# Three edits around the slot loop: the order of GpSimd's diagonal adds, and where TensorE waits for a slot's low parts

## The reference

```python
x = x + einsum('bct,bcd->bdt', x, L0_weights[itok_B_0_15])      # 64x64 mix of the rows, one of 16
x = x + einsum('bct,bcd->bdt', x, L1_weights[itok_B_0_15])      # the same, other weights
x = x + einsum('bsi,oi->bso', x, W) + low_rank(x, lora_A[itok_B_0_2], lora_B_w) * 0.5
x = x + einsum('bsi,boi->bso', x, L3_weight[itok_B_3_7])        # 1024x1024 adapter, one of 8
```

## Time and profile before

| | us |
|---|---|
| median of 3 runs | 383.75 |
| lowest and highest | 383.16, 384.0 |
| the profiled execution, time of the run | 384.77 |
| its span, first to last instruction | 383.0 |
| granted TensorE clock, mean | 0.999 |

### The profile page before, as it was taken

One profiled execution on the slowest core, in us unless ns is written; L12 is line 12 of the kernel. 1 busy time (PEld: TensorE's weight loads), 2 busy tenths in 40 slices (PEclk: granted clock), 3 DMA queues, 4 the chain that ended last, 5 costly groups with the idle time before them and its releaser, 6 DMA issues.

```text
span 383.0 us, 7652 instructions
## 1 busy us (share of the span) xinstructions
PE 376.4 (98%) x1733; PEld 312.9 (82%) x1734; DVE 267.6 (70%) x301; ACT 225.5 (59%) x299; POOL 115.3 (30%) x157
## 2 busy tenths in 40 slices
PE   8999999999999999999999999999999999999995
PEld 7888888888888888888888888778888888888784
DVE  3796977847849788447968458844599635999653
ACT  3689577487247375244474565753677536778443
POOL 0000230100000000024765356663167532566600
PEclk9999999999999999999999999999999999999999
DMA  8975905630378294406528226542256522664223
GB/s 276 399 284 206 344 0 181 236 133 7 106 269 287 103 329 152 171 9 220 159 73 267 63 51 203 205 125 59 56 187 200 169 58 58 205 228 123 60 62 86
DMA packets 24187, 61.38 MB, mean 160 GB/s; under 512 B 1906, under 2 KB 2098, under 8 KB 24114
## 3 DMA queue, kind: packets, MB, share of 16 engines
q1 hardware_dynamic: 23648, 60.10, 47.6%
q10 hardware_dynamic: 466, 0.44, 0.3%
HBM read 52.15 MB, written 8.39 MB: 158 GB/s over the span
## 4 chain that ended last, share of the span: by engine, by line
PE 97%; DMA 1%; issue 0%; DVE 0%; ACT 0%
PE ps L1514 45%; PE ps L1373 12%; PE ps L1374 12%; PE ps L1375 12%; PE ps L1400 4%; PE ps L1537 4%; PE ps L1439 3%; PE ps L1602 2%; PE ps L1412 2%; DMA ring_f<-xt 1%; PE ps L1552 1%; PE ps L1449 0%; DVE ring L878 0%; ACT stage L850 0%
## 5 line engine op out<-in xcount | busy, mean ns | idle before, releaser
L1514 PE MATMUL ps<-ring,aT 128*128 x752 | 173.7, 390 | 0.5 <-issue 0.5
L1514 PEld LDWEIGHTS ps<-ring,aT 128*128 128x128 f32 x752 | 140.9, 188 | 30.8 <-issue 1.7
L1373 PE MATMUL ps<-ring 128*128 128x512 f32 x208 | 81.1, 390 | 0.0
L1374 PE MATMUL ps<-ring 128*128 128x512 f32 x208 | 81.0, 389 | 0.0
L1375 PE MATMUL ps<-ring 128*128 128x512 f32 x208 | 80.9, 389 | 0.0
L476 POOL TENSOR_TENSOR aT<-xT,aT 128x512 fp32r<-128x512 f32 (+1 forms) x36 | 56.4, 1587 | 46.3 <-ACT aT L761 43.1
L1266 DVE TENSOR_TENSOR ring<-raw,ring 128x1024 f32 (+1 forms) x40 | 62.6, 1623 | 6.2 <-ACT ring L747 6.2
L767 ACT ACTIVATE aT<-ps 64x1024 fp32r<-64x1024 f32 x32 | 32.7, 1023 | 47.1 <-PE ps L1514 46.7
L1294 DVE TENSOR_TENSOR stage<-ps,stage 64x1024 f32<-64x1024 f32 x30 | 36.7, 1222 | 29.4 <-ACT stage L776 28.7
L1283 DVE TENSOR_TENSOR aT<-ps,aT 64x1024 fp32r<-64x1024 f32 x32 | 39.1, 1223 | 21.6 <-ACT aT L767 20.9
L1375 PEld LDWEIGHTS ps<-ring 128*128 128x128 f32 x208 | 39.1, 188 | 8.2
(11 more groups left out here) (95 smaller groups left out, 328.6 us busy)
## 6 DMA issues: line engine op xcount, KB each, us to landing
raw<-w3t SPq DMA_DIRECT2D x40, 512.0 KB, 4.4
ring_f<-xt SPq DMA_DIRECT2D x8, 1024.0 KB, 8.4
raw<-xt SPq DMA_DIRECT2D x8, 1024.0 KB, 5.3
out<-stage SPq DMA_DIRECT2D x30, 256.0 KB, 3.2
ring_f<-wt SPq DMA_DIRECT2D x4, 1024.0 KB, 8.1
xT<-xt SPq DMA_DIRECT2D x3, 1024.0 KB, 10.4
xT<-wt SPq DMA_DIRECT2D x2, 1024.0 KB, 16.0
ring_f<-wt SPq DMA_DIRECT2D x4, 256.0 KB, 5.1
```

Of the source, the lines that this page charges most:

```text
L1373: pe.matmul(dst, hi_of(qw)[:, k, cs], hi_of(qx)[:, k, :], start=start and k == 0, stop=False, skip_group_check=True)
L1374: pe.matmul(dst, hi_of(qw)[:, k, cs], lo_of(qx)[:, k, :], start=False, stop=False, skip_group_check=True)
L1514: last = pe.matmul(acc(i)[:, n, :], x3_split(i, k, start, P), ring[:, bass.ds(off + (part * D + n * 512), 512)], start=(k == 0 and j == 0) ...
```

## The change

Two functions change. In GpSimd's `step`, the adds for MORE of slot i are no longer made in step i but in step i+1, after `slot_lo(i+2)` and `mixers(i+1)`; the adds for LOAD_A stay in their step (those of slot 0 are made in step 1, as before), and come after those for MORE where a step has both. On TensorE, `slot_ready` of slots 1 and on waits for the slot's high parts (`s_hi`) and no longer for its low parts; the wait for the low parts (`s_lo`) stands now ahead of the first matmul of tile 0 that reads them: the third pass of a pair, which is after 4 matmuls, and the first pass of a single batch.

```diff
-                for w in ([], [earlier, word])[i] if i < 2 else [word]:
-                    with pool.If(get(w, LOAD_A) > 0):
-                        adapter_eyes(HALF, pool.snap(get(w, THIS)))
-                    with pool.If(get(w, MORE) > 0):
-                        adapter_eyes(0, pool.snap(get(w, THIS) + 1))
+                if i == 1:
+                    with pool.If(get(earlier, LOAD_A) > 0):
+                        adapter_eyes(HALF, pool.snap(get(earlier, THIS)))
+                if i:
+                    with pool.If(get(earlier, MORE) > 0):
+                        adapter_eyes(0, pool.snap(get(earlier, THIS) + 1))
+                    with pool.If(get(word, LOAD_A) > 0):
+                        adapter_eyes(HALF, pool.snap(get(word, THIS)))
                 return word, following
@@ products, on TensorE
                     for j, (start, part) in enumerate(passes):
+                        if i and k == 0 and start + P > P and j == (len(passes) - 1 if start == P else 0):
+                            pe.wait_ge(s("s_lo"), 2 * i + 4)
                         for n in range(2):
@@ slot_ready, on TensorE
-                pe.wait_ge(s("s_lo"), 2 * i + 4 if i else 2)
+                if i:
+                    pe.wait_ge(s("s_hi"), 2 * i + 4)
+                else:
+                    pe.wait_ge(s("s_lo"), 2)
```

## The result

| kernel | median us | lowest to highest | runs |
|---|---|---|---|
| before | 383.75 | 383.16 to 384.13 | 5 |
| changed | 395.05 | 393.93 to 395.80 | 5 |

A forecast was written before the change was run, and what follows sets the result against it. TensorE, busy 98% of the span, was taken as the bound, so stalls count in full. Two places at 2.76 us plus 1.87 at slot 6's made 7.4, added to the 383.75 median: 391.2 us, range 388.4 to 394.6.

The forecast's parts named there:

- the three waits: TensorE's mixes in slots 6, 10 and 14 wait for `rows_lo`, a stall of 2.76 us each.
- the clock: Rival: TensorE's clock falls after each stall, 24 matmuls at half speed, 5.44 us more per place, 407.5 us; chance 0.03.
- The queue behind the adds: Steps 5, 9, 13: ScalarE's copies start 5.2 us later; VectorE's low parts, sum and `rows_lo` follow, ending at T+19.25.
- What would show it: Predicted trace signs: no gap at slot 6's head, three mix waits of 2 to 3 us, ScalarE waiting some 5 us.
- The contention given back: VectorE's four low parts take 4.64 us instead of 7.14, no longer beside GpSimd's `slot_lo`; 2.5 us back.
- The 0.7 us between `rows_lo` and the mix: Lead needed from the end of VectorE's `rows_lo` to an undisturbed TensorE mix: about 0.7 us.
- The gain at slot 6: The gap at slot 6's head goes, 0.89 us at most, leaving +1.87 us at that place.
- the loss at slot 15: The mix at slot 15, about 0.3 us too late before the change, was to stay so.
- Lateness swallowed by VectorE's slack: Rival: mixes not delayed and slot 6's gap goes, 382.9 us; chance 0.07.
- VectorE staying slow at 7.14: Rival: four low parts still cost up to 7.14 us, up to 2.5 more per place, 394 to 398.7; chance 0.09.
- One place escapes: Rival: one or two of the three places show no stall, 2.8 us less each, 385.6 to 388.4; chance 0.09.
- its terms, -0.15 to +0.4 and up to +1.1: Range allowances in us: lead before the mix of 0.55 to 1.1, and low parts of 1.14 to 1.44 each.

The follow-up runs named there:

- experiment 8: The kernel before, unchanged, run once more for a second trace: one run of 384.89 us.
- experiment 2: Against the kernel before: only TensorE's later wait for the low parts, GpSimd in its old order; 383.9 us, ratio 1.0002.
- experiment 4: Changed kernel plus two float32 matmuls adding zero on TensorE ahead of the mix waits in slots 6, 10 and 14; 391.32 us.
- experiment 9: Changed kernel with `mixed_cols` and `mixed_sum` ahead of the adapter tiles in steps 5, 9 and 13 alone; 387.58 us.
- experiment 3: Changed kernel with the moved adds between the low parts of x and the four small copies; 384.85 us.
- experiment 1: Changed kernel with GpSimd's new order only, TensorE waiting for the low parts at the slot's begin as before; 394.44 us.
- experiment 6: Changed kernel with the adds moved in one place only (MORE of slot 4, made in step 5); 386.68 us.
- experiment 5: Changed kernel with `mixed_cols` and `mixed_sum` ahead of the adapter tiles in every step; 391.67 us.
- experiment 7: Changed kernel with four fills of unused scratch on GpSimd ahead of the moved adds in steps 5, 9 and 13; 406.26 us.

## Why the prediction was wrong where it was

I forecast 391.2 us, range 388.4 to 394.6; it is 395.05. The sign was right, with a chance of 0.92, and so was the mechanism of the three waits. The step that failed is the clock, which the sum has at nothing. By its steps:

- **The queue behind the adds: right, within 0.1 us.** Counted from the start of ScalarE's step 5 (237.21), the first add began at 7.75 (said: 7.77), ScalarE's copies at 8.33 (8.4), VectorE's low parts at 9.56 (9.6) and took 4.63 us (4.64), `rows_lo` ended at 19.21 (19.25). What would show it, as I listed it, was there: three waits of the mix in slots 6, 10 and 14, ScalarE waiting some 5 us for line 468, and no gap at slot 6's head.
- **The contention given back: right.** Four low parts took 4.63 us without GpSimd beside them and 7.14 with it. By the rule of the Trainium skill's page "SBUF — State Buffer", section "Who interferes with whom", that I had weighed, the two exclude each other; the trace of after agrees, with 4.63 at all three moved places.
- **The 0.7 us between `rows_lo` and the mix: mis-sized.** It was read from places where the mix was hardly late. A mix that already waits started 0.22 us after `rows_lo` and lost 0.27 us in its four matmuls: 0.49, below the 0.55 to 1.1 I allowed, and a place costs 2.51 to 2.53 us, not 2.76.
- **The gain at slot 6: wrong.** I took 0.89 us off one place since the trace showed that gap, and measured it against the median. The trace was of an execution of 384.77 us, 1.0 us above the median, and the second trace shows the gap at another slot (experiment 8). Against that one trace the term holds; in the median no such gain is seen (experiment 2). The sum should have been 3 x 2.76 = 8.3 us; measured are 7.7 (experiment 4). Nor did the loss at slot 15 stay, as I had said: its mix took 0.91 us without a gap (371.35).
- **The clock: wrong in its chance and its price.** This is what put the result outside the range. The sum takes the clock as unchanged. I gave a fall a chance of 0.03 and a price of 5.44 us per place, as if 24 matmuls had to run at half speed, and my argument against it was that the trace of before shows no fall; but it shows no gap of that size either, so it was no evidence. Measured: a fall after two of three gaps in both traces, 1.6 us each, and 3.1 to 3.7 us in the median. Over the five runs the span goes with the mean clock: 394.0 us of span at 0.987, 392.1 to 392.4 at 0.991. With what was measured afterwards for both terms the sum is 383.75 + 7.7 + 3.4 = 394.9.
- **The rivals.** Lateness swallowed by VectorE's slack: experiment 9 shows how near it was, with the sum out of the way, and experiment 3 at 384.85 how early the adds would have had to be. VectorE staying slow at 7.14: no. One place escapes: no.

So the forecast was 3.9 us too low: the clock's 3.1 to 3.7 and the 0.9 of slot 6 were missing, and the three places had been put 0.7 too high. The range doesn't add up as written either: its terms, -0.15 to +0.4 and up to +1.1, taken at each of the three places, reach from 390.7 to 395.7, where I wrote 390 to 395 and cut the top to 394.6. That top would have held 395.05, but by luck: it stands on slower low parts and a longer lead, and neither came.

## What to carry to other kernels

Where TensorE is busy for 98% of the span, moving a step later on a side engine costs its lateness less the slack of the longest queue behind it; go through that queue to the next thing TensorE waits for, and count contention that ends. A gap of TensorE of 2 us or more can have a second price, as it had here, the clock after it, and a trace without gaps can't tell you that it is absent. A gap of half a microsecond that one trace shows at one place is not yet a gain to be had: look first how that execution stands to the median, and take a second trace.

## What the runs showed of the hardware

- Gaps of 2.25 us made the granted clock fall towards 0.5 afterwards in two places of three in two traces (changed kernel and experiment 1), and in one execution of six with a single gap (experiment 6); a gap of 2.44 us was followed by a fall in the one trace that has it (experiment 5), and gaps of 4.4 to 4.5 us by one each time (experiment 7). Gaps of 0.3 to 0.54 us (experiments 3, 4 and 9), one of 1.21 us (experiment 9, slot 15's head) and one of 1.59 us (experiment 7, slot 15's mix) were followed by no slow stretch in their traces. A fall after a gap of 2.25 or 2.44 us cost 1.6 us each time, after the longer gaps 1.6, 2.4 and 2.6, the two larger where it had come during the gap. The Trainium skill's page "TensorE: Matmul & The Clock Gate", section "HAM oscillation — how this bites in real kernels", says that idle gaps throttle the engine again; the traces here agree, though not every gap of 2.25 us did it.
- After a gap of 2.25 us the low clock was met by TensorE at work: the stretch 300 to 307 us of the changed kernel, which holds the whole second gap, has a granted clock of 1.00, and 307.50 to 310.90 has 0.53.
- Two float32 matmuls of 512 columns took 1.72 us, and put in each of the three gaps they were cheaper than nothing: 391.32 us with them, 394.44 (experiment 1, timed beside it) and 395.05 without.
